# Second attention: scores from two float32r parts, two heads in the two halves of the rows

## The chip, the core and the metric

The kernel runs on one core of one Trainium2 chip, in one launch. The metric is the device time of that launch in microseconds; less is better. Before the change it is 2244.51 us (median of 3 runs, 2242.51 to 2246.36).

## What is computed

Four residual blocks run on a tensor of 4 x 1024 tokens x 128 features. The third, which the change touches, is causal attention with 16 heads of 8 dimensions; the others are a gated memory (before it) and two feed-forward blocks with local attention (one before it, one after).

```python
x = x + attn_a(_layernorm(x)); x = x + ffn(_layernorm(x))
x = x + attn_b(_layernorm(x)); x = x + ffn(_layernorm(x))

def attn_b(x):                        # 4 x 1024 x 128, H = 16 heads, DK = 8
    Q, K, V = (split_heads(x @ W.T) for W in (Wq, Wk, Wv))
    Q, K = apply_rope(Q, cos, sin), apply_rope(K, cos, sin)
    logits = einsum('bhnd,bhmd->bhnm', Q, K) / sqrt(DK)
    probs = softmax(where(causal, logits, -inf), axis=-1)
    attn = einsum('bhnm,bhmd->bhnd', probs, V)
    return merge_heads(attn) @ Wo.T
```

The scores are large enough that queries and keys rounded once to bf16 would not do; softmax also needs each row's maximum.

## The kernel before, in words

`network` runs five stages one behind the other; the second attention is `attn_b_stage`, from 893 to about 1502 us of the profiled execution. Its engines have a program each, joined by semaphores.

**Parts.** The projections and the rotation give f32 queries and keys, 128 rows (16 heads x 8 dimensions) x 1024 tokens for each of 4 batches. Each value is split into three bf16 parts (`PARTS = 3`): ACT copies to bf16 (`first_part`), DVE or POOL subtracts (`remainder`), ACT copies again (`second_part`), DVE or POOL subtracts again (`third_part`). The parts go to DRAM (`store_parts`, `store_first_rows`) and come back (`load`) so that all nine products of parts are rows of one contraction: `KS9` = 3 x 3 x 8 = 72 rows of `QS` and `KS`. Three more rows hold the three bf16 parts of minus the row maximum in `QS`, and ones in `KS`, so that 75 rows give score minus maximum.

**Steps.** Work goes in 16 groups (`NG`) of 4 heads (`BG`). Step n has eight slots j, one for each tile of 128 keys. In slot j four things run side by side:

- exponentials (`exp_unit`, L1684): scores of keys tile j against queries from tile j on, transposed, into one of two buffers of 1024 columns (`s2_ps`); ACT takes exp of it into `PT` (L1867). A group has 22 such units.
- values (`value_block`, L1702): `PT` of slot j-1 times [V, 1], f32, four heads in four column groups of 32, in one or two halves of 512 queries. For n < 3 the causal cut is a mask matmul ahead of the scores (L1679); from n = 3 (`SELECTS`) POOL cuts in `PT` (L2080), and the value block waits for it.
- maxima for a later group (`max_unit`, L1652): scores of one query tile against its keys, at most 512 columns, into one of two banks (`s1_ps`); DVE reduces each with max (L1956). The causal cut is a mask matmul of 128 columns ahead of the scores (L1649). A group has 38 units. `MAX_TILES` puts query tiles 4, 7, 6, 5 in slots 0 to 3 and 3, 2, 1, 0 in slots 4 to 7.
- offsets: after slot 3 DVE joins the two halves of the maxima (`maximum`), POOL splits them in bf16 parts in four operations (`offsets`), in slot 5 PE turns them (`turn_unit`, L1661), DVE copies them to `MT`, and one DMA on SP writes the three rows of `QS` (`rows`, L1532). The first exponential of the next step waits for it.

Each engine runs its instructions in the order in which the loops write them. On PE, `step` spreads a slot's maxima evenly behind its exponentials and value blocks (`some_maxima`); a maximum that waits for its bank holds back every exponential and value block behind it. SP issues the outputs' DMAs (`store_out`, two times eight a step), `rows` and, once a group is done, `load` of the group three ahead (`RING` = 3), six DMAs.

## Time and profile before

| | |
|---|---|
| runs | 2242.51, 2244.51, 2246.36 us, median 2244.51 |
| the profiled execution | span 2242.3 us from the first to the last instruction |
| its granted TensorE clock | 0.973 of 2.4 GHz on average |
| second attention | 893 to about 1502 us |
| first exponential, last step | 980.2 us, 1465.4 us |

The span is the profiled execution's own time as far as the profile records it; what lies around it is not in the profile, and the median of the runs is 2.2 us above it. An engine's busy time is what its instructions took; matmuls overlap, and a matmul's recorded duration includes its latency, so PE's pace is read from the starts. PEclk is the granted clock, 1.00 for 2.4 GHz and 0.50 for 1.2 GHz.

### The profile page before, as it was taken

The page shows a single profiled execution, that of the slowest core. Times are in us where ns is not written, and L with a number is a line of the kernel's source. Part 1 is how long each engine was busy: PE and PEld are TensorE (multiplying, and loading weights), DVE is VectorE, ACT ScalarE, POOL GpSimd, SP SyncE. Part 2 cuts the span into 40 slices and gives each one's busy share as a digit, 9 for nine tenths or more (in the row PEclk, how much of TensorE's full clock was granted, in tenths as well). Part 3 has the DMA queues.
Part 4 walks back from the last instruction along what each step waited for, and adds up shares of the span by engine and source line. Part 5 has one row for each costly group of instructions (what it writes and reads, how often), then busy time and mean ns, then how long its engine had stood idle before and what let it go on. Part 6 is the DMA issues. An engine that isn't in the chain of part 4 may idle for free. (4 is left out here: it accounts for less than half of the span.)

```text
span 2242.3 us, 44709 instructions
## 1 busy us (share of the span) xinstructions
PE 2064.8 (92%) x16567; PEld 1059.9 (47%) x16567; DVE 1792.0 (80%) x2386; ACT 1390.5 (62%) x3475; POOL 1233.3 (55%) x633
## 2 busy tenths in 40 slices
PE   5677899999999997899999999967999999999997
PEld 2224555555555553443333333314555555555554
DVE  6986889899899993666777777717899899899993
ACT  8455566666666664446666666665666756766663
POOL 0217777777777772135121221128777787777770
PEclk9899999999999999889999999999999999999998
DMA  2004112112112110402111111113111111111111
GB/s 62 0 6 121 35 34 47 35 34 48 35 36 47 35 34 19 130 29 88 55 48 52 54 36 46 32 55 87 31 43 42 35 44 39 34 44 39 35 34 43
DMA packets 86075, 101.14 MB, mean 45 GB/s; under 512 B 13817, under 2 KB 59841, under 8 KB 83557
## 3 DMA queue, kind: packets, MB, share of 16 engines
q1 hardware_dynamic: 83429, 96.58, 16.8%
q8 instruction: 135, 2.21, 0.4%
q10 hardware_dynamic: 2432, 1.70, 0.3%
q14 instruction: 79, 0.65, 0.1%
HBM read 35.98 MB, written 8.39 MB: 20 GB/s over the span
## 5 line engine op out<-in xcount | busy, mean ns | idle before, releaser
L831 POOL TENSOR_TENSOR ffn_RN<-ffn_SS,ffn_mhalf 128x16 f32<-128x16 f32 x128 | 372.5, 2910 | 279.3 <-DVE ffn_SS L777 278.9
L1956 DVE TENSOR_REDUCE attn_b_NX<-attn_b_s 128x1 f32<-128x512 f32 (+3 forms) x608 | 381.3, 660 | 132.0 <-PE attn_b_s L1652 126.8
L825 POOL TENSOR_TENSOR ffn_QK<-ffn_T 128x1024 f32<-128x1024 f32 x128 | 421.6, 3294 | 17.6 <-DVE ffn_T L725 17.4
L576 ACT ACTIVATE ffn_PB<-ffn_s,ffn_NM 128x128 f32<-128x128 f32 x1024 | 360.8, 386 | 101.1 <-DVE ffn_NM L747 101.1
L1867 ACT ACTIVATE attn_b_PT<-attn_b_s 128x1024 f32<-128x1024 f32 (+3 forms) x352 | 298.2, 870 | 192.4 <-PE attn_b_s L1684 188.0
L612 ACT ACTIVATE ffn_SQ<-ffn_w 128x1024 f32<-128x1024 f32 x128 | 131.2, 1025 | 312.0 <-DVE ffn_T L725 311.7
L819 POOL TENSOR_TENSOR ffn_PB<-ffn_PB,ffn_RDEN 128x1024 f32<-128x1024 f32 x128 | 243.7, 1904 | 25.1 <-DVE ffn_RDEN L710 25.1
L367 PE MATMUL ffn_w<-ffn_Wqkv,ffn_H 128*128 128x512 f32 x512 | 244.2, 600 | 10.4 <-ACT ffn_SQ L612 4.7
L576 ACT ACTIVATION_READ_ACCUMULATOR ffn_PB<-ffn_s,ffn_NM 128x1 f32 x1024 | 231.0, 226 | 0.0
L1652 PE MATMUL attn_b_s<-attn_b_KS,attn_b_QS 72*128 72x512 bf16 (+3 forms) x768 | 220.6, 336 | 6.2 <-DVE attn_b_NX L1956 5.5
L741 DVE TENSOR_TENSOR ffn_QK<-ffn_QK,ffn_RN 128x1024 f32<-128x1024 f32 x128 | 222.4, 1738 | 0.4 <-POOL ffn_RN L831 0.3
L764 DVE COPY ffn_PT<-ffn_w 128x1024 f32<-128x1024 f32 x128 | 156.2, 1220 | 76.1 <-PE ffn_w L421 72.6
L2080 POOL TENSOR_SCALAR_AFFINE_SELECT attn_b_PT<-attn_b_PT 128x512 f32<-128x512 f32 x104 | 66.8, 642 | 252.6 <-ACT attn_b_PT L1867 251.4
L1684 PE MATMUL attn_b_s<-attn_b_QS,attn_b_KS 75*128 75x512 bf16 (+3 forms) x768 | 186.9, 333 | 5.9 <-ACT attn_b_PT L1867 4.8
L442 PE MATMUL ffn_m<-ffn_HN,ffn_W 128*114 128x512 f32 x360 | 185.9, 613 | 6.4 <-ACT ffn_G L596 3.7
L722 DVE TENSOR_TENSOR ffn_T<-ffn_w,ffn_rope 128x1024 f32<-128x1024 f32 x128 | 154.8, 1210 | 36.6 <-PE ffn_w L367 36.4
L1702 PE MATMUL attn_b_o<-attn_b_PT,attn_b_VQ 128*32 128x512 f32 (+3 forms) x1536 | 166.2, 505 | 3.8 <-POOL attn_b_PT L2080 3.5
L725 DVE TENSOR_TENSOR ffn_T<-ffn_w,ffn_rope 128x512 f32<-128x512 f32 x256 | 163.7, 681 | 0.0
L747 DVE TENSOR_REDUCE ffn_NM<-ffn_s 128x8 f32<-128x1024 f32 x128 | 155.6, 1215 | 9.6 <-PE ffn_s L409 9.6
L774 DVE TENSOR_REDUCE ffn_SS<-ffn_SQ 128x16 f32<-128x1024 f32 x128 | 154.6, 1208 | 2.2 <-ACT ffn_SQ L612 2.2
L437 PEld LDWEIGHTS ffn_w<-ffn_PT,ffn_Voff 128*64 128x64 f32 x2048 | 107.3, 137 | 100.7 <-issue 94.4
L421 PEld LDWEIGHTS ffn_w<-ident,ffn_PB 128*128 128x128 f32 x1024 | 117.4, 143 | 75.4 <-issue 60.5
(257 smaller groups left out, 3756.4 us busy)
## 6 DMA issues: line engine op xcount, KB each, us to landing
ffn_Voff<-ffn_Vcur SPq DMA_DIRECT2D x248, 128.0 KB, 2.3
attn_b_QS<-attn_b_qk_parts SPq DMA_DIRECT2D x48, 192.0 KB
attn_b_KS<-attn_b_qk_parts SPq DMA_DIRECT2D x48, 192.0 KB
ffn_H<-ffn_Y SPq DMA_DIRECT2D x64, 128.0 KB, 2.5
ffn_H<-ffn_U SPq DMA_DIRECT2D x64, 128.0 KB, 2.5
attn_b_qk_parts<-attn_b_RP SPq DMA_DIRECT2D x6, 768.0 KB, 4.3
ffn_rope<-in_ffn_rope_dram SPq DMA_DIRECT2D x4, 1024.0 KB, 7.9
attn_b_rope<-attn_b_OS SPq DMA_DIRECT2D x252, 16.0 KB
```

Of the source, the lines that this page charges most:

```text
L367: last = pe.matmul(w0_ps[:, c, :], H1[:, g % 2, b, :], Wqkv[:, l, c, :], start=True, stop=True)
L442: pe.matmul(mlp_bank(g, half, j), W1[:, g // NT, half, j, :], HN[:, :], start=True, stop=True)\
L576: last = act.activation(PB[:, x % 2, e, p, :], s_ps[:, e, p * P:(p + 1) * P], ACT.Exp, bias=NM[:, x % 2, e, p:p + 1], accum_out=DEN[:, x % ...
L741: dve.tensor_tensor(qk, qk, RN[:, x % 2, :].unsqueeze(2).broadcast_to([P, 2 * NH, DH]), ALU.mult)\
L819: pool.tensor_tensor(probs_x, probs_x, by, ALU.mult).then_inc(normed, 1)
L825: pool.tensor_tensor(QK[:, x % 2, :, :, :].rearrange("p c q k -> p (c q k)"), T1[:, :, :, :].rearrange("p c h k -> p (c h k)"), T2[:, :, : ...
L831: pool.tensor_tensor(RN[:, x % 2, :], SS[:, x % 2, :], mhalf[:, :], ALU.pow).then_inc(rnorm, 1)
L1652: last = pe.matmul(bank[:, q * width:(q + 1) * width], QS[0:KS9, m % RING, g + q, i * P:(i + 1) * P], KS[0:KS9, m % RING, g + q, lo:hi], s ...
L1684: last = pe.matmul(bank[:, q * pitch + lo:q * pitch + hi], KS[:, n % RING, g + q, j * P:(j + 1) * P], QS[:, n % RING, g + q, j * P + lo:j ...
L1702: last = pe.matmul(o_ps[half][VCOLS * g:VCOLS * (g + 1), lo - half * 512:512], VQ[:, n % 2, g, j, :], PT[:, j % 2, g, lo - j * P:hi - j * ...
L1867: act.activation(PT[:, j % 2, g:g + pack, 0:width], s2_ps[k % 2][:, 0:pack * pitch].rearrange("p (q w) -> p q w", q=pack)[:, :, 0:width], ...
L1956: dve.tensor_reduce(NX[:, m % 2, c, g:g + pack, i], s1_ps[k % 2][:, 0:pack * (hi - lo)].rearrange("p (q w) -> p q w", q=pack), AX_X, ALU.m ...
```

## The change

Queries and keys are split into two parts of 12 bits in the type float32r (`PARTS = 2`): an ACT copy and one subtraction. The four products of parts are 4 x 8 = 32 rows (`TERMS`), and a second head gets the other 64 rows (`NPAR` = 2 halves, `HROWS` = 64, `NPR` = 2 heads in each half, four heads a group as before). Rows 32 to 61 of each half are filled with ones in `KS` and zeros in `QS`; rows 62 and 63 hold the two parts of minus the maximum. The maxima use 62 rows of a half, the exponentials all 64. The causal masks are matmuls on one half of the rows too, two of 64 columns a head where one of 128 was. An exponential's unit is now one half of the queries (512 columns or less) for two or four heads, one bank for each half of the rows: 20 units instead of 22. The maxima keep 38 units. `rows` takes four DMAs, `load` eight. The core of the diff:

```diff
-PARTS = 3
-KS9 = PARTS * PARTS * BD
+PARTS = 2
+TERMS = PARTS * PARTS * BD
+NPAR, NPR = 2, 2
+HROWS = P // NPAR
+OFFSETS = HROWS - PARTS
...
-        RP = sb("RP", [P, 2, PARTS, T], BF16)
+        RP = sb("RP", [P, 2, PARTS, T], F32R)
-        QS = sb("QS", [KS9 + PARTS, RING, BG, T], BF16)
-        KS = sb("KS", [KS9 + PARTS, RING, BG, T], BF16)
+        QS = sb("QS", [P, RING, NPR, T], F32R)
+        KS = sb("KS", [P, RING, NPR, T], F32R)
...
             def rows(m):
                 sp.wait_ge(s1_read, s1_at["turn", m] + 1)
-                sp.dma_start(QS[KS9:KS9 + PARTS, m % RING, :, :].rearrange("a g t -> a (g t)"), MT[:, m % 2, :])\
-                  .then_inc(s_rows[m % 2], 16)
+                for par in range(NPAR):
+                    for a in range(PARTS):
+                        at = par * HROWS + OFFSETS + a
+                        of = (a * NPAR + par) * NPR * NT
+                        sp.dma_start(QS[at:at + 1, m % RING, :, :].rearrange("a q t -> a (q t)").bitcast(F32),
+                                     MT[of:of + NPR * NT, m % 2, :]).then_inc(s_rows[m % 2], 16)
...
+            def mask(at, par, kind, half, n, first):
+                rows = rows_for(par, HROWS)
+                pe.matmul(at, causal[rows, kind, half, 0:P],
+                          causal[rows, kind, half:half + 1, P:P + HROWS].broadcast_to([HROWS, n, HROWS]), start=first,
+                          stop=True, skip_group_check=True)
...
+            def max_unit(m, slot, u):
...
+                if diagonal:
+                    at = bank[:, 0:n * width].rearrange("p (q w) -> p q w", q=n)
+                    for half in range(2):
+                        lo = width - P + half * HROWS
+                        mask(at[:, :, lo:lo + HROWS], par, 0, half, n, half == 0)
+                rows = rows_for(par, OFFSETS)
+                for q, (i, c, pr) in enumerate(segments):
+                    last = pe.matmul(bank[:, q * width:(q + 1) * width], QS[rows, m % RING, pr, i * P:(i + 1) * P],
+                                     KS[rows, m % RING, pr, c * 512:c * 512 + width], start=not diagonal, stop=True,
+                                     skip_group_check=True)
...
+            def exp_unit(n, j, u):
...
                 for q in range(pack):
-                    for lo in range(0, width, 512):
+                    for par in range(NPAR):
+                        rows = rows_for(par, HROWS)
+                        last = pe.matmul(bank[par][:, q * width:(q + 1) * width],
+                                         KS[rows, n % RING, first + q, j * P:(j + 1) * P],
+                                         QS[rows, n % RING, first + q, lo:hi], start=not masked and q == 0, stop=True,
...
-            def second_part(b, w):
-                act.wait_ge(r1, 2 * b + w + 1)
-                act.activation(RP[:, w, 1, :], work_buffers(b, w)[0], ACT.Copy).then_inc(p2, 1)
...
+            for par in range(NPAR):
+                at = par * HROWS + TERMS
+                pool.wait_ge(s_set, 2 * par + 1)
+                pool.memset(KS[at:(par + 1) * HROWS, :, :, :].bitcast(F32), 1.0).then_inc(s_set, 1)
+                pool.wait_ge(s_set, 2 * par + 2)
+                pool.memset(QS[at:par * HROWS + OFFSETS, :, :, :].bitcast(F32), 0.0).then_inc(s_set, 1)
```

## Rows read from the trace of the kernel before

**Rows 1.** The page, part 1: busy us of each engine, share of the span, instructions.

```profile
span 2242.3 us, 44709 instructions
...
PE 2064.8 (92%) x16567; PEld 1059.9 (47%) x16567; DVE 1792.0 (80%) x2386; ACT 1390.5 (62%) x3475; POOL 1233.3 (55%) x633
```

**Rows 2.** Windows of the eight slots of one step: busy us per engine, then PE clock.

```profile
1244.54:1248.74 4.20, 3.86 (x29) 1.41 (x27) 3.38 (x5) 3.56 (x4) 0.56 (x2) 1.00 0.27 68
1248.74:1254.80 6.06, 5.87 (x40) 1.88 (x37) 4.55 (x8) 4.26 (x6) 1.44 (x3) 1.00 0.50 163
1254.80:1260.72 5.92, 5.49 (x37) 1.81 (x36) 4.74 (x9) 3.25 (x4) 0.63 (x1) 1.00 0.10 20
1260.72:1265.65 4.93, 4.75 (x37) 1.71 (x35) 4.27 (x7) 2.71 (x4) 0.63 (x1) 1.00 0.00 0
1265.65:1269.18 3.53, 3.53 (x31) 1.24 (x28) 2.79 (x5) 2.05 (x2) 1.35 (x5) 1.00 0.00 0
1269.18:1272.37 3.19, 2.96 (x22) 1.09 (x21) 1.93 (x5) 2.00 (x3) 0.88 (x2) 1.00 0.01 3
1272.37:1274.52 2.15, 2.15 (x19) 0.97 (x18) 1.69 (x3) 1.02 (x1) 0.46 (x2) 1.00 0.20 38
1274.52:1275.90 1.38, 1.38 (x19) 0.73 (x17) 0.69 (x1) 0.60 (x1) 0.50 (x2) 1.00 0.13 24
```

**Rows 3.** Timeline of PE, slot 1: start us, us, line, tiles, form, [idle].

```profile
1250.03 1.06 PE L1702 MATMUL attn_b_o<-attn_b_PT,attn_b_VQ 128*32 128x512 f32 x8
1251.03 0.61 PE L1652 MATMUL attn_b_s<-attn_b_KS,attn_b_QS 72*128 72x512 bf16 x2
...
1252.20 0.23 PE L1649 MATMUL attn_b_s<-attn_b_causal,identb 128*128 128x128 bf16 x1 [0.19 <-DVE attn_b_NX L1956]
1252.27 0.38 PE L1652 MATMUL attn_b_s<-attn_b_KS,attn_b_QS 72*128 72x512 bf16 x1
```

**Rows 4.** Timeline of DVE at the same place, with its idle time.

```profile
1251.45 2.58 DVE L1956 TENSOR_REDUCE attn_b_NX<-attn_b_s 128x1 f32<-128x512 f32 x4 [0.63 <-PE attn_b_s L1652]
```

**Rows 5.** Timeline of ACT, slot 0.

```profile
1245.18 3.77 ACT L1867 ACTIVATE attn_b_PT<-attn_b_s 128x1024 f32<-128x1024 f32 x4 [1.00 <-PE attn_b_s L1684]
```

**Rows 6.** Groups of instructions from 893 to 1502 us: busy, mean ns, idle.

```profile
L1956 DVE TENSOR_REDUCE attn_b_NX<-attn_b_s 128x1 f32<-128x512 f32 (+3 forms) x608 | 381.3, 660 | 132.0 <-PE attn_b_s L1652 126.8
```

**Rows 7.** Timeline of PE in the feed-forward stage before.

```profile
701.16 0.41 PE L400 MATMUL ffn_s<-ffn_masks,identb 64*64 64x512 bf16 x4
...
706.28 1.88 PE L367 MATMUL ffn_w<-ffn_Wqkv,ffn_H 128*128 128x512 f32 x4
```

**Rows 8.** Tile view of the score banks: weight loads, min/median/max ns.

```profile
L1652 PEld LDWEIGHTS attn_b_s<-attn_b_KS,attn_b_QS x768: 95/98/152, 931.4 to 1457.7; 72*128 72x128 bf16 x192
...
L1591 PEld LDWEIGHTS attn_b_s<-attn_b_XN,attn_b_W x64: 186/190/337, 900.6 to 969.5; 128*128 128x128 f32 x64
...
L1661 PEld LDWEIGHTS attn_b_s<-identb,attn_b_NP x16: 119/119/123, 975.6 to 1460.5; 128*96 128x96 bf16 x16
```

**Rows 9.** Windows where the clock fell: PE, PEld, DVE, ACT, POOL, PEclk.

```profile
972.00:976.00 4.00, 2.78 (x18) 1.23 (x16) 3.00 (x6) 1.09 (x2) 3.77 (x7) 0.99 0.00 0
976.00:980.00 4.00, 3.73 (x16) 1.43 (x17) 3.03 (x6) 0.00 (x0) 3.92 (x2) 0.50 0.03 6
1048.00:1052.00 4.00, 3.35 (x29) 1.59 (x27) 2.69 (x4) 3.15 (x4) 2.72 (x2) 1.00 0.14 25
980.00:1012.00 32.00, 31.47 (x188) 12.18 (x186) 21.70 (x36) 18.66 (x22) 4.59 (x7) 0.80 0.01 1
1045.00:1077.00 32.00, 30.43 (x213) 12.05 (x210) 21.50 (x35) 20.00 (x25) 9.45 (x8) 0.89 0.30 96
```

**Rows 10.** Timeline of the SP queue after one offset turn.

```profile
1270.75 0.78 SPq L1532 DMA_DIRECT2D attn_b_QS<-attn_b_MT  x1
```

**Rows 11.** The page, part 6: DMA issues, KB each, us to landing.

```profile
ffn_Voff<-ffn_Vcur SPq DMA_DIRECT2D x248, 128.0 KB, 2.3
```

**Rows 12.** Timeline of POOL at the stage's start.

```profile
893.87 1.80 POOL L2015 MEMSET attn_b_VQ<- 128x2048 f32 x1
```

More of the change, by code:

```diff
@@ L12 @@
 F32 = mybir.dt.float32
+F32R = mybir.dt.float32r
 BF16 = mybir.dt.bfloat16
@@ L1448, in last_max, with last_exp @@
         def last_max(m):
-            i, c, g, pack = max_units(MAX_SPLIT - 1)[-1]
-            return s1_at[m, i, c, g]
-        def last_exp(n, j):
-            return s2_at[n, j, exp_heads(j)[-1][0]]
+            slot = MAX_SPLIT - 1
+            return s1_at[m, slot, len(max_units(slot)) - 1]
+        def last_exp(n, j, half=1):
+            return max(s2_at[n, j, u] for u, unit in enumerate(exp_units(j)) if unit[0] <= half)
         def work_buffers(b, w):
@@ L1669, in exp_unit @@
+                pe.matmul(s1_ps[k % 2][0:PARTS * BG * NT, 0:P],
+                          NP[:, m % 2, :, :, :, :].rearrange("p a g h i -> p (a g h i)").bitcast(F32),
+                          keep["ident"][:, :], start=True, stop=True).then_inc(s1_mm, 1)
+            def exp_unit(n, j, u):
+                k = s2_at[n, j, u]
+                half, first, pack = exp_units(j)[u]
+                lo, hi = piece(j, half)
+                width = hi - lo
                 wait(pe, probs, k - 1)
-                if (n, j, g) == (0, 0, 0):
+                if (n, j, u) == (0, 0, 0):
@@ L1671, in exp_unit @@
                     pe.wait_ge(held, 4 * (NB - 2))
-                if (j, g) == (0, 0):
-                    pe.wait_ge(s_rows[n % 2], 16 * (n // 2 + 1))
-                each = max(1, 512 // pitch)
-                selected = n >= SELECTS
-                for q in range(0, 0 if selected else pack, each):
-                    at = bank[:, q * pitch:q * pitch + each * min(pitch, 512)]\
-                        .rearrange("p (q w) -> p q w", q=each)[:, :, 0:P]
-                    pe.matmul(at, keep["identb"][:, :], causal[:, 1:2, :].broadcast_to([P, each, P]), start=True,
-                              stop=True)
@@ L1724, in step @@
                     halves = list(range(j // 4, 2)) if 0 <= v < NG else []
-                    pieces, done = len(heads) + len(halves), 0
+                    pieces, done = len(exps) + len(halves), 0
                     def some_maxima(done):
-                        for unit in scores[len(scores) * done // pieces:len(scores) * (done + 1) // pieces]:
-                            max_unit(m, *unit)
+                        for u in range(len(scores) * done // pieces, len(scores) * (done + 1) // pieces):
+                            max_unit(m, slot, u)
@@ L1738, in step @@
                             value_block(v, j, halves[0])
                             done = some_maxima(done)
-                        if halves and k == len(heads) - 1:
+                        if halves and u == len(exps) - 1:
                             value_block(v, j, halves[-1])
                             done = some_maxima(done)
-                    if not heads:
-                        for unit in scores[:1]:
-                            max_unit(m, *unit)
+                    if not exps:
+                        for u in range(len(scores))[:1]:
+                            max_unit(m, slot, u)
@@ L1746, in step @@
                         if slot == TURN_SLOT and n == -1:
                             turn_unit(0)
-                        for unit in scores[1:]:
-                            max_unit(m, *unit)
+                        for u in range(len(scores))[1:]:
+                            max_unit(m, slot, u)
                             if m == 0:
@@ L1798, in hold @@
                 else:
[L1799 removed]
+                    act.wait_ge(lower, 2 + w + 1)
                 for i in range(2):
@@ L1821, in _ @@
             first_part(0, 1)
-            for w in range(2):
-                second_part(0, w)
             for c in range(4, 6):
@@ L1834, in _ @@
             hold(2, 0)
-            for w in range(2):
-                second_part(1, w)
             hold(2, 1)
@@ L1871, in _ @@
+                if pack > 1:
+                    bank = bank.rearrange("p r (q w) -> p r q w", q=pack)
+                    out = out.rearrange("p (q r) w -> p r q w", r=NPAR)
+                act.activation(out, bank, ACT.Exp).then_inc(probs, 1)
             for n in range(NG):
                 for j in range(NT):
-                    for g, pack in exp_heads(j):
-                        exp_unit(n, j, g, pack)
-                        if (j, g) == (1, 0) and n >= 1:
+                    for u in range(len(exp_units(j))):
+                        exp_unit(n, j, u)
+                        if (j, u) == (1, 0) and n >= 1:
@@ L1942, in _ @@
             remainder(1)
-            for w in range(2):
-                third_part(w)
             for c in range(4, NCH):
@@ L2045, in parts_of @@
                     remainder(b, w)
-                for w in range(2):
-                    third_part(b, w)
             def values(m):
```

291 lines of the change are left out of this document (147 added, 144 removed).

## Prediction, made before the changed kernel was run

> **What bounds the kernel now.** Read the page first [rows 1]: the span is 2242.3 us, PE is busy 92% of it and DVE 80%. That average is over stages the change does not touch, so the next views are of the second attention alone, 893 to 1502 us. Cut one step of it at the starts of its eight slots and the windows give 4.20, 6.06, 5.92, 4.93, 3.53, 3.19, 2.15 and 1.38 us, 31.36 us in all [rows 2]. PE is busy 29.99 us of these, DVE 24.05, ACT 19.45. Busy PE means little, as overlapping ends are counted; what counts is from start to start. The timeline shows two score matmuls of 512 columns started in 0.44 us, 0.22 each; a causal mask of 128 columns takes 0.07 before its score matmul starts; a value block (eight f32 instructions, four heads in four column groups) takes 1.00 us [rows 3]. By these, a step's 36 tiles of 128 columns times 4 heads are 18432 columns, at 2.4 GHz 7.7 us for the maxima and 7.7 us for the exponentials; masks 22 x 0.07 and more for wide ones, some 1.8; value blocks 9.5: 512 columns in four passes are 0.85 us of the 1.00, and with the other 0.15 kept the narrower ones take 0.79, 0.58 and 0.36 (six, two, two and two of them). For the turn into each of the 12 blocks I put 0.1, an estimate from that 0.15: 1.2. Sum 27.9 of 31.36: PE is close to its limit, and DVE (38 reductions, 0.66 us mean [rows 6]) close behind. The engines are coupled: the maxima have two banks, and while PE is in a value block DVE runs dry. It waits 0.63 us after one [rows 4]; in slots 1 to 3 DVE is busy 13.56 of 16.91 us, so 3.35 us is such waiting. Slot 0 is different: four exponentials of 1024 in 3.77 us [rows 5] fill the 4.20 us, so ACT sets it.
>
> **The change, part by part.**
> The exponentials' scores (L1684). 48 matmuls a step stay 48, but neighbours work on different halves of the rows and on different banks. Whether halves overlap is seen one stage earlier: four 64x512 matmuls on quarters of the array start within 0.24 us, where one alone needs 0.21 [rows 7]. So a pair takes one matmul's time, and 7.7 us becomes 3.85. The float32r rate is in no row. Ends: the bf16 row, 0.22 us for 512 columns [rows 3]; and f32, where two products of 512 columns take four instructions and 1.88 us [rows 7], some 0.9 each with the last one's latency, four times bf16. 
>
> The maxima's scores (L1652). Still 38 units and 48 matmuls, each unit one half of the rows. Two units overlap only when both banks are free, which DVE seldom lets happen: I take no gain (0 to 3.8 us a step).
>
> Weight loads. A 128-column bf16 load lasts 95 ns, a 96-column one 119, an f32 one 186 [rows 8]: 128 columns of bf16 are loaded faster than fewer. If a float32r load loses that, it adds about 40 ns, half the distance from 95 to 186. Beside a 512- or 256-column matmul this is hidden; beside 64-column masks and 128-column matmuls it isn't. Each diagonal maximum now has two masks of 64 columns a head in place of one of 128, so another load too. I take 55 ns for each diagonal unit, between nothing and 2 x 70 (two mask rows [rows 3]); slots 4 to 7 have 12 of them, and slot 7 has one unit more than before: 13 x 0.055 = 0.7 us. In slots 1 to 3 the ten others lie beside DVE.
>
> The Trainium skill, "TensorE: Matmul & The Clock Gate" (LDWEIGHTS, and Weight-path perf modes), speaks against the change: a load takes its columns over 1.2 GHz, 107 ns, with the fast form for none of the 4-byte types. A pair of 512 columns then needs 214 ns of loads beside 213 ns of columns, so pairs of 384, 256 and 128 columns also take 214: the exponentials would take 24 x 0.214 = 5.1 us, not 3.85, and the gain per step be 1.2 us smaller. The 24 ns between the 96- and the 128-column load agree that bf16 has a faster form; what a float32r load costs, no row shows.
>
> Slot by slot. Slot 0: ACT still has four of 1024, 4.20 to 4.10. Slots 1 to 3: each wait of DVE behind a value block had an exponential's matmuls in it, and PE now arrives earlier at the block. What is left is the block's 1.00 plus about 0.4 us to the first new maximum, less the two maxima that DVE holds, of which one is begun: about 0.4 us where it was 0.63. Six blocks then leave 2.05 us of the 3.35: gain 1.3, ends 0 and 3.35. Slots 4 to 7: PE sets them (busy 10.02 of 10.25 us); the exponentials have 4 x (512 + 384 + 256 + 128) = 5120 columns, 2.13 us, half goes: 1.07 less 0.7 for masks and loads, gain 0.37. Together 0.1 + 1.3 + 0.37 = 1.77 us a step. The 15 steps that still have maxima beside them make 26.5 us; the last one is set by ACT, with 20 exponentials in place of 22, and I take nothing.
>
> ACT and DVE. The same 18432 columns in 20 instructions instead of 22: under 0.4 us of ACT a step, not on the path but in slot 0. DVE keeps 38 reductions. The second minimum is smaller, the turned offsets are 64x128 f32 instead of 96x128 bf16: nothing.
>
> The offsets' way. One DMA becomes four on SP. It is issued in 0.78 us at 1270.75 [rows 10]; the next step's first exponential, which waits for it, starts near 1275.9, 5.2 us on. Such a transfer inside the chip lands 2.3 us after its issue [rows 11]; the last of four then lands at 0.78 x 3 + 2.3 = 4.6 us, beside about 5.0 in the shorter slots. Nothing, ends 0 and 1 us a step. Queued behind them on SP are eight DMAs of outputs and the loads, eight instead of six of nearly equal bytes (2 x 64 rows x 8 KB against 2 x 72 rows x 8 KB); these are needed over ten microseconds later. POOL's offset work goes from four operations to two: hidden before, hidden now.
>
> Lead-in. Second and third parts go: eight ACT copies, two DVE and six POOL subtractions. PE and the norm's chain set the time there, and DVE has slack, so nothing, ends 0 and -3 us. New are four memsets of 6144 elements on 30 or 32 rows: at 1.80 us for 2048 [rows 12] 5.4 us each, 21.6 in series, done by about 918, before POOL's first other work at 923. Nothing, ends 0 and +3. The stored parts grow from 768 to 1024 KB each; nobody waits that closely.
>
> Sum: 2242.3 - 26.5 = 2215.8 us of span. The median of the runs is 2.2 us over this span, which I take to lie around it, giving 2218.
>
> **The rivals.**
> The clock falls. A PE that starts its columns sooner and then waits for DVE and ACT is less active, above all in slot 0: four pairs (0.9), four maxima (0.9) and a value block (0.4) in 4.1 us. The clock went to 1.2 GHz after stretches with waits here: 972 to 976 us has PE busy 2.78 of 4 and the next four have 0.50; 1048 to 1052 has 3.35 of 4 at ACT's pace, and the 32 us around it have a mean of 0.89 against 1.00, so 7.0 us at half; 980 to 1012 has 0.80, 12.8 us at half [rows 9]. Then PE sets the pace and loses half of that, 3.5 to 6.4 us for a fall. Against it: no fall in the steady steps before, and pairs use all the rows. It decides from a fall in half of the steps (1.77 / 3.5) on; one in each step gives 15 x (3.5 - 1.77) = +26, 2270, and with 6.4 +69, 2314.
>
> Short float32r matmuls are slow. If those of 128 columns cost as f32, 0.16 us more each: eight maxima and eight exponentials in four pairs a step, up to 12 x 0.16 = 1.9 us, ten of them (1.6) in slot 7 where nothing covers it. 15 x (1.6 - 1.77) = -3: 2242. For: f32's price by column; against: nothing.
>
> Float32r takes more passes. With two, 3.85 us more for the exponentials than forecast, 7.7 for the maxima: PE needs 27.9 - 3.85 + 11.5 + 0.7 = 36.3 us a step, +4.9 x 15 = 74: 2318; with four some 2650.
>
> The halves don't overlap (the change does not do what it says): PE's sum stays at 27.9, plus 0.7 + 0.3: +15, 2260. Against it the quarters [rows 7].
>
> **How the numbers follow.** Forecast 0.52; clock 0.22; short ones 0.12; passes 0.08; no overlap 0.06. About 0.2% (4.5 us) is what a measurement of this kernel tells from none. The forecast is faster for 0.50 and same for 0.02; the clock rival slower for 0.15, same 0.03, faster 0.04; short ones faster 0.05, same 0.04, slower 0.03; the last two slower for 0.13, same 0.01. Faster 0.59, same 0.10, slower 0.31. The forecast's own range is 2196 (3.2 us a step) to 2236. The whole range goes on to 2280 and leaves out the passes, the clock at its dearest and a gain over 3.2 us a step.
>
> **What would show it.** In the changed trace: pairs of L1684's successor starting together, 0.21 us apart from the next; float32r forms of 512 columns lasting as the bf16 ones; loads near 135 ns; steps of about 29.6 us; DVE's waits halved and its 38 reductions unchanged; PEclk 1.00 in the steady steps; no wait of slot 0 for the offsets' DMA. A PEclk of 0.5 in every step, a third column of matmul time on 128-column forms, or a step above 31.4 us would make it wrong.

## The result, and the profile after

The changed kernel takes 2319.11 us, the median of four runs from 2296.53 to 2330.83; the kernel before took 2245.44 beside it. The ratio is 1.0302, 95% interval 1.0271 to 1.0333: slower by 3%, where 2218 was forecast and 2280 was the upper end. The rows of "after" are of the slowest of its runs: 2330.83 us, span 2329.1, mean clock 0.937. The fastest run had a span of 2294.8 at 0.957; the spread goes with the clock.

The page after: busy time of each engine, and the groups of DVE's reductions and ACT's exponentials (busy us, mean ns, idle us before them).

```profile
PE 2103.7 (90%) x16998; PEld 1112.5 (48%) x16998; DVE 1793.5 (77%) x2383; ACT 1378.6 (59%) x3435; POOL 1235.7 (53%) x599
...
L1974 DVE TENSOR_REDUCE attn_b_NX<-attn_b_s 128x1 f32<-128x512 f32 (+3 forms) x608 | 384.0, 660 | 210.8 <-PE attn_b_s L1677 205.2
...
L1892 ACT ACTIVATE attn_b_PT<-attn_b_s 128x1024 f32<-128x1024 f32 (+1 forms) x320 | 292.5, 940 | 279.0 <-PE attn_b_s L1710 276.9
```

The 608 reductions are the same, 660 ns each, but DVE stood idle before them 210.8 us instead of 132.0 [rows 6], almost all of it for the maxima's scores. PE's busy time has risen by 39 us although the two halves' matmuls overlap. So something makes PE later, and the windows say what. A step is cut here from one copy of the turned offsets to the next. First the 15 steps of after in one line, then single steps of it; the columns are those of [rows 9].

```profile
982.08:1544.91 562.83, 499.28 (x3671) 220.56 (x3671) 370.23 (x608) 294.38 (x341) 99.91 (x149) 0.83 0.16 40
...
1134.47:1169.86 35.39, 30.38 (x240) 13.32 (x240) 24.24 (x40) 19.20 (x23) 5.93 (x11) 0.90 0.16 39
...
1242.13:1285.45 43.32, 39.43 (x240) 16.69 (x240) 24.48 (x40) 19.14 (x23) 5.97 (x11) 0.65 0.13 32
1285.45:1318.94 33.49, 28.30 (x240) 12.68 (x240) 24.32 (x40) 19.14 (x23) 5.97 (x11) 1.00 0.17 41
```

And the 15 steps of before:

```profile
975.90:1460.89 484.99, 464.95 (x3268) 170.93 (x3268) 366.60 (x609) 301.03 (x375) 115.14 (x183) 0.98 0.17 48
```

The steps take 77.8 us more, of 86.8 in the whole span (the lead-in 6.2 more, the rest what comes behind). There are two losses. **Pace:** at a clock of 1.00 a step takes 33.2 to 33.5 us (35.5 in the two that also hold a batch's output projection, 33.3 before), where it took 31.4. That is 2 us a step, 30 in all. **Clock:** eleven of the 15 steps contain a stretch at 1.2 GHz. By 562.83 x (1 - 0.83) x 2 it is 191 us of half clock, against some 20 before. One step at 0.65 takes 9.8 us more than its neighbour at 1.00, one at 0.90 takes 2. That leaves the clock some 48 of the 77.8 us, as what the pace doesn't take; in a run of the median time it is some 12 us less.

The slots of one step at full clock, from windows in the manner of [rows 2], for before, for before with half of the exponentials' columns left out (experiment 3), for after, and for after in bf16 (experiment 2):

| slot | 0 | 1 | 2 | 3 | 4 | 5 | 6 | 7 | sum |
|---|---|---|---|---|---|---|---|---|---|
| before | 4.20 | 6.06 | 5.92 | 4.93 | 3.53 | 3.19 | 2.15 | 1.38 | 31.36 |
| before, half the columns | 3.76 | 5.99 | 5.92 | 4.90 | 3.44 | 3.18 | 2.15 | 1.23 | 30.57 |
| after | 3.87 | 6.43 | 6.45 | 4.93 | 4.18 | 3.72 | 2.10 | 1.80 | 33.48 |
| bf16 in halves | 3.54 | 6.14 | 5.97 | 4.52 | 3.74 | 3.24 | 2.05 | 1.51 | 30.71 |

Four of these windows of after:

```profile
1291.29:1295.16 3.87, 2.82 (x26) 1.38 (x24) 2.32 (x5) 3.00 (x4) 0.28 (x1) 1.00 0.13 24
1295.16:1301.59 6.43, 5.87 (x45) 2.39 (x43) 4.99 (x8) 4.75 (x6) 1.56 (x3) 1.00 0.50 129
...
1312.97:1317.15 4.18, 3.50 (x34) 1.22 (x31) 3.45 (x6) 2.05 (x2) 1.28 (x4) 1.00 0.01 2
...
1322.97:1324.77 1.80, 1.80 (x29) 1.30 (x25) 1.20 (x3) 0.60 (x1) 0.42 (x2) 1.00 0.12 22
```

Against before, slot 0 of after gained, every other slot but 3 and 6 lost, and no engine is full in most of them: in slots 4 and 5 PE is busy 6.66 of 7.90 us, DVE 5.45. PE, DVE and ACT wait for one another in turn. The timeline of PE shows what makes a turn longer. First after, then the bf16 version at the same place of a step:

```profile
1477.63 0.50 PE L1710 MATMUL attn_b_s<-attn_b_QS,attn_b_KS 64*128 64x512 f32 x2 [0.88 <-ACT attn_b_PT L1892]
1477.97 0.40 PE L1677 MATMUL attn_b_s<-attn_b_KS,attn_b_QS 62*128 62x512 f32 x1
...
1485.67 0.49 PE L1677 MATMUL attn_b_s<-attn_b_KS,attn_b_QS 62*128 62x512 f32 x2
1485.99 0.40 PE L1710 MATMUL attn_b_s<-attn_b_QS,attn_b_KS 64*128 64x256 f32 x4
1486.93 0.50 PE L1677 MATMUL attn_b_s<-attn_b_KS,attn_b_QS 62*128 62x512 f32 x1 [0.54 <-DVE attn_b_NX L1974]
```

```profile
1150.46 0.39 PE L1677 MATMUL attn_b_s<-attn_b_KS,attn_b_QS 62*128 62x512 bf16 x2
1150.68 0.39 PE L1710 MATMUL attn_b_s<-attn_b_QS,attn_b_KS 64*128 64x256 bf16 x4
1151.62 0.39 PE L1677 MATMUL attn_b_s<-attn_b_KS,attn_b_QS 62*128 62x512 bf16 x1 [0.55 <-DVE attn_b_NX L1974]
```

The pair of the two halves is one line, x2, in 0.50 us: both ran together, so the halves do overlap. A matmul whose load was done before it started takes 0.40, as one of bf16 (0.38 in [rows 3]): the columns run at the bf16 rate. But one that follows a wait takes 0.50, where bf16 takes 0.39, and its load is recorded as starting with it. Experiments 2, 5 and 13 test whether the 0.11 us are this load. In the step of 33.49 us, 50 of the 96 score matmuls are recorded at least 0.05 us longer than any of their form in bf16, in 32 places when neighbours are counted together: 6 right after an idle PE, 4 after a value block, 17 after a mask, the rest after another matmul. PE itself is idle for over 0.06 us only 12 times in that step. The loads of after, on PEld:

```profile
1475.57 0.30 PEld L1677 LDWEIGHTS attn_b_s<-attn_b_KS,attn_b_QS 62*128 62x128 f32 x2
1475.68 0.29 PEld L1710 LDWEIGHTS attn_b_s<-attn_b_QS,attn_b_KS 64*128 64x128 f32 x2
1475.79 0.30 PEld L1677 LDWEIGHTS attn_b_s<-attn_b_KS,attn_b_QS 62*128 62x128 f32 x2
...
1477.63 0.19 PEld L1710 LDWEIGHTS attn_b_s<-attn_b_QS,attn_b_KS 64*128 64x128 f32 x2 [1.31 <-ACT attn_b_PT L1892]
...
1485.64 0.20 PEld L1677 LDWEIGHTS attn_b_s<-attn_b_KS,attn_b_QS 62*128 62x128 f32 x2
```

The profile writes float32r as f32. One float32r load lasts 0.18 to 0.19 us. Two on the same half take 0.30, so they follow each other 0.11 us apart; two on different halves fit in 0.19 or 0.20. The 0.11 us agree with the Trainium skill, "TensorE: Matmul & The Clock Gate" (LDWEIGHTS, and Weight-path perf modes): a load takes its columns over 1.2 GHz, and FP32 has no fast form. Float32r behaves here as the Trainium skill has it for FP32.

### The profile page after: what moved, and what is told of

Same layout as the page of the kernel before. It is cut to its first block and busy times, and to the rows that moved or that the text cites. A ratio compares the mean times of both kernels' runs of the same rounds, so it can differ in the third digit from the quotient of the medians.

```text
span 2329.1 us, 45562 instructions
## 1 busy us (share of the span) xinstructions
PE 2103.7 (90%) x16998; PEld 1112.5 (48%) x16998; DVE 1793.5 (77%) x2383; ACT 1378.6 (59%) x3435; POOL 1235.7 (53%) x599
## 5 line engine op out<-in xcount | busy, mean ns | idle before, releaser
L1974 DVE TENSOR_REDUCE attn_b_NX<-attn_b_s 128x1 f32<-128x512 f32 (+3 forms) x608 | 384.0, 660 | 210.8 <-PE attn_b_s L1677 205.2
L1892 ACT ACTIVATE attn_b_PT<-attn_b_s 128x1024 f32<-128x1024 f32 (+1 forms) x320 | 292.5, 940 | 279.0 <-PE attn_b_s L1710 276.9
L1677 PE MATMUL attn_b_s<-attn_b_KS,attn_b_QS 62*128 62x512 f32 (+3 forms) x768 | 267.1, 464 | 22.3 <-DVE attn_b_NX L1974 21.8
L1710 PE MATMUL attn_b_s<-attn_b_QS,attn_b_KS 64*128 64x512 f32 (+3 forms) x768 | 193.4, 432 | 15.7 <-ACT attn_b_PT L1892 15.6
L1727 PE MATMUL attn_b_o<-attn_b_PT,attn_b_VQ 128*32 128x512 f32 (+3 forms) x1536 | 197.5, 591 | 5.2 <-POOL attn_b_PT L2091 5.1
L1677 PEld LDWEIGHTS attn_b_s<-attn_b_KS,attn_b_QS 62*128 62x128 f32 x768 | 126.5, 214 | 100.3 <-DVE attn_b_NX L1974 79.2
```

The source lines that it names most:

```text
L1677: last = pe.matmul(bank[:, q * width:(q + 1) * width], QS[rows, m % RING, pr, i * P:(i + 1) * P], KS[rows, m % RING, pr, c * 512:c * 512 + ...
L1710: last = pe.matmul(bank[par][:, q * width:(q + 1) * width], KS[rows, n % RING, first + q, j * P:(j + 1) * P], QS[rows, n % RING, first + q ...
L1727: last = pe.matmul(o_ps[half][VCOLS * g:VCOLS * (g + 1), lo - half * 512:512], VQ[:, n % 2, g, j, :], PT[:, j % 2, g, lo - j * P:hi - j * ...
L1892: act.activation(out, bank, ACT.Exp).then_inc(probs, 1)
L1974: dve.tensor_reduce(at, bank, AX_X, ALU.max, negate=True).then_inc(s1_read, 1)
```

## The experiments

Each ran beside the kernel before, whose median was 2244.0 to 2246.2 us. "Step" is a step at full clock without an output projection unless its clock is given. A fence under an experiment is one step of it, with the columns as above. The steps are of the one profiled run, the times of all its runs.

**1. Score matmuls of the exponentials run twice** (nothing else is changed).

```diff
-                for q in range(pack):
+                for q in [*range(pack)] * (1 if masked or n < SELECTS else 2):
```

> The changed kernel with every score matmul of the exponentials issued twice in groups 3 to 15 (the second pass overwrites the first with the same values): 3.8 us of matmul more in each of 13 steps. Theory 'clock' (the changed kernel's steps are slow because PE is idle more and the clock is at 1.2 GHz for about 187 us of the stage): PE is active again, the clock stays at 1.00 in nearly all steps after the third, and although it does more work the kernel gets faster, 2265 to 2290 us. Theory 'loads' (each float32r matmul costs more, the clock is a side effect): the extra matmuls and loads add 1.5 to 4 us a step, 2335 to 2370 us.

2292.8 us (2285.49 to 2308.54), ratio 1.0217 [1.0171, 1.0263]: 26 us less than the changed kernel, with 48 more matmuls a step.

```profile
1224.17:1258.21 34.04, 31.26 (x288) 16.39 (x288) 24.41 (x40) 19.22 (x23) 5.96 (x11) 1.00 0.17 40
```

In the profiled run (2286.66 us) the step is longer by half a microsecond to 0.9 us, and every step from the third on is at 1.00; two of the four runs were 12 to 22 us longer at a lower mean clock. So part of the loss is the clock's, and more matmuls on PE take it back. With 'loads' alone the time would have risen.

**2. The changed kernel in bf16** (two bf16 parts in the same halves, rows and order; the scores then carry 16 bits only).

```diff
-F32R = mybir.dt.float32r
+F32R = mybir.dt.bfloat16
...
```

> The changed kernel with the two parts in bf16 in place of float32r (the scores carry 16 bits and no more), the same halves of rows, masks and units; half the bytes in the loads. Theory 'loads': a bf16 weight load is hidden again, steps at a clock of 1.00 take 30 us or less instead of 33.3. Theory 'clock': PE is even less busy, so the falls stay or grow: a mean clock in the steps of 0.85 or less, and the kernel stays slower than before, 2260 to 2310 us. If loads were all of it: 2200 to 2225 us.

2235.21 us (2232.06 to 2236.23), ratio 0.9949 [0.9934, 0.9964], 0.5% faster than before.

```profile
1135.75:1166.46 30.71, 25.06 (x239) 7.76 (x237) 23.65 (x42) 21.29 (x27) 5.97 (x11) 1.00 0.12 28
```

The type costs 2.4 to 2.8 us a step (with it go half of the loads' bytes and the f32 turn of the offsets). Nearly all falls of the clock go too, although PE is busy less here; that part of the expectation missed.

**3. The kernel before with half of the columns of the exponentials' scores** (from group 3 on; it leaves the other half of these scores out).

```diff
+                        if selected:
+                            hi = lo + (hi - lo) // 2
```

> The kernel before with only the first half of the columns of each score matmul of the exponentials computed from group 3 on: leaves out half of these scores. It takes PE time out as the change does (3.8 us a step) but keeps bf16, 75 rows, one mask a unit, all waits. Theory 'clock': less work for PE brings falls of the clock here too, PEclk under 0.95 in the steps and a time of 2250 us or more, although work was taken away. Theory 'loads': the clock stays at 1.00 and 13 steps gain 1.5 to 2 us each: 2215 to 2225 us.

2236.6 us (2232.82 to 2239.61), ratio 0.9958 [0.9943, 0.9972].

```profile
1112.22:1142.79 30.57, 27.37 (x217) 10.39 (x215) 23.78 (x41) 19.40 (x25) 6.49 (x13) 1.00 0.17 50
```

This is the gain of the change without anything else of it: 3.8 us of columns out of PE shorten a step by 0.8 us, and slots 4 to 7, which lose 1.07 us of columns, by 0.25. The time is neither of the two that I had put. The forecast had 2.47 for this alone: its 1.77 and the 0.7 that it charged for masks and loads. The clock stayed, on 72 and 75 rows.

**4. The maxima's mask as one matmul on all rows** in place of two on a half.

```diff
-                    for half in range(2):
-                        lo = width - P + half * HROWS
-                        mask(at[:, :, lo:lo + HROWS], par, 0, half, n, half == 0)
+                    pe.matmul(at[:, :, width - P:width], keep["identb"][:, :],
+                              lower_mask[:, :, :].broadcast_to([P, n, P]), start=True, stop=True)
```

> The changed kernel with the maxima's causal cut as before the change: one mask matmul of 128 columns over all 128 rows, in place of two of 64 columns on one half of the rows. 22 matmuls and loads fewer a step, but PE turns between all rows and half the rows ahead of and behind each diagonal unit. If the doubled masks are what made a step at full clock 2 us longer, such steps take 32.3 us or less instead of 33.3. If the float32r loads are, they stay within 0.5 us of 33.3, or get longer by the turns. Total 2290 to 2330 us by both, as the clock's falls stay.

2421.94 us (2410.45 to 2440.08), ratio 1.079 [1.0736, 1.0845].

```profile
1326.76:1383.10 56.34, 54.80 (x218) 21.84 (x218) 25.23 (x41) 19.29 (x22) 5.95 (x11) 0.50 0.10 25
...
1523.50:1559.45 35.95, 33.50 (x218) 14.82 (x218) 24.82 (x41) 19.14 (x23) 6.00 (x11) 1.00 0.16 39
```

Fewer matmuls (218 for 240), yet 2.5 us more at full clock, some 0.11 for each of the 22 masks. In its trace a score matmul starts 0.16 us behind such a mask, where it is 0.07 in the changed kernel, and its load starts no earlier. The Trainium skill, "TensorEngine Tiling (Array Packing)" (Key Properties), says that a change of the tiling mode drains the engine; the run agrees. The clock fell further too (three steps at 0.50 throughout), so the whole is some 90 us over the 2290 to 2330 that I had put. The changed kernel's split masks were the better choice.

**5. The maxima's 512-column matmuls in two of 256** (24 more float32r loads a step, each beside columns).

```diff
-                    last = pe.matmul(bank[:, q * width:(q + 1) * width], QS[rows, m % RING, pr, i * P:(i + 1) * P],
+                    step_by = 256 if width == 512 else width
+                    for x in range(0, width, step_by):
+                        last = pe.matmul(bank[:, q * width + x:q * width + x + step_by],
...
```

> The changed kernel with each 512-column score matmul of the maxima issued as two of 256 columns: same columns, 24 float32r weight loads more in a step (for 512-column segments). Theory 'loads' (a float32r matmul's weight load, 0.18 us recorded against 0.095 for bf16, is not hidden and costs about 0.11 to 0.13 us each): a step at full clock goes from 33.4 to 35 us or more, and the total by 20 us or more beyond 2319. Rival 'columns' (the loads are hidden, float32r columns stream slower than bf16): steps at full clock stay at 33.4 within 0.5.

2320.71 us (2297.7 to 2323.76), ratio 1.0312 [1.0262, 1.0362]; step 33.20 us, as in the changed kernel. A load beside 256 columns costs nothing that can be seen. So loads in general are not the price of the type; what is left is the load that nothing covers.

**6. Experiment 2 with half of the exponentials' columns from group 3 on** (these scores left out).

```diff
+                        cut = width if n < SELECTS else width // 2
-                        last = pe.matmul(bank[par][:, q * width:(q + 1) * width],
+                        last = pe.matmul(bank[par][:, q * width:q * width + cut],
...
```

> The bf16 variant of the halves with only the first half of the columns of each exponential's score matmul computed from group 3 on (leaves out half of these scores): 1.9 us of PE's columns less a step. Theory 'density' (the clock falls in the changed kernel because the same columns are spread over steps of 33.4 instead of 30.7 us, so PE computes less of the time): taking columns out brings the falls to bf16 too, PEclk 0.95 or less in several steps, total 2240 to 2290. Rival 'type' (float32r matmuls themselves bring the falls): the clock stays near 1.00, steps stay near 30.6, total 2228 to 2236.

2313.78 us (2311.63 to 2314.51), ratio 1.0302 [1.0286, 1.0317].

```profile
1144.47:1184.02 39.55, 33.76 (x239) 9.21 (x237) 24.29 (x42) 21.24 (x27) 6.00 (x11) 0.61 0.09 22
```

Less work than in experiment 2 and 79 us more time, with the clock down to 0.54 to 0.95 in all 12 steps that it changes. So in these halves the clock falls with fewer columns in bf16 too, and further than I had put (2240 to 2290).

**7 and 8. The filled rows left out**, in float32r and in bf16: 33 and 35 rows of each half in the scores instead of 62 and 64.

```diff
-OFFSETS = HROWS - PARTS
+OFFSETS = TERMS + 1
...
-                        rows = rows_for(par, HROWS)
+                        rows = rows_for(par, OFFSETS + PARTS)
```

> The changed kernel with 33 rows of each half for the maxima and 35 for the exponentials (offsets moved down to rows 33 and 34), instead of 62 and 64. If the filled rows do nothing, steps and clock are as in the changed kernel, 2297 to 2331 us. If they keep the clock up, the clock is lower in every step, a mean in the steps of 0.75 or less, and the time is 2350 us or more.

> The kernel with the halves in bf16, with 33 and 35 rows of a half in the scores in place of 62 and 64 (the filled rows are left out, nothing else). 'Filled rows hold the clock up' whatever the type: the clock falls in most steps, steps of 40 us or more, 2370 to 2500 us. 'It was float32r's': the time stays near 2235 us.

2532.91 us (2530.41 to 2534.73), ratio 1.1278 [1.1261, 1.1295], and 2430.69 (2425.62 to 2438.24), ratio 1.0821 [1.0795, 1.0847]. One step of each kernel:

```profile
1229.78:1279.64 49.86, 46.58 (x240) 20.27 (x240) 24.66 (x40) 21.58 (x27) 5.95 (x11) 0.50 0.12 28
```

```profile
1372.51:1416.99 44.48, 40.95 (x239) 10.42 (x237) 24.40 (x42) 21.42 (x28) 5.92 (x11) 0.50 0.08 19
```

Every step ran at half clock or close to it (0.50 to 0.53, and 0.50 to 0.62 in bf16). Where the clock is up, a bf16 matmul of 512 columns lasts 0.37 to 0.39 us on 33, 35, 62 or 64 rows, so the rows of zeros and ones cost no time; leaving them out costs about 14 us a step in bf16, by the clock.

**9. Half-width kernel with all three bf16 parts** (six of the nine products of parts: 48 rows, 13 filled, three of offsets; the three smallest products are left out).

```diff
-PARTS = 2
-TERMS = PARTS * PARTS * BD
+PARTS = 3
+TERMS = PARTS * (PARTS + 1) // 2 * BD
```

> Two heads in the two halves of the rows, but with three bf16 parts as before the change and six of their nine products (the three smallest left out): 48 rows, filled to 61, and three offset rows. By 'loads', steps like the bf16 variant's, 30.7 us at full clock, and the clock up: 2230 to 2242 us, faster than the kernel before (2245) with all three parts kept. If the halves as such are what costs, 2260 us or more.

2238.78 us (2236.19 to 2243.68, seven runs), ratio 0.9972 [0.9961, 0.9984] to before; step 30.71 us, four with a short fall. The change's packing without its type is 0.3% faster than the kernel before.

**10. One more load behind each wait of experiment 2** (32 columns on the same weights, 38 maxima and both halves of 20 exponentials).

```diff
+                pe.matmul(bank[:, 0:32], QS[rows, m % RING, pr, i * P:(i + 1) * P],
+                          KS[rows, m % RING, pr, c * 512:c * 512 + 32], start=True, stop=True, skip_group_check=True)
...
```

> The kernel with the halves in bf16 (steps of 30.71 us at full clock, where the float32r kernel needs 33.2 to 33.5), with one more matmul of 32 columns on the same weights behind every wait for a bank: at the start of each of the 38 maxima and, from group 3 on, of each exponential's two halves. So each wait is followed by a bf16 load of some 95 ns more, about what a float32r load (182 to 188 ns) has over a bf16 one. 'The exposed load' (the 2.5 us of a full-clock step that float32r costs are its longer load behind each wait, 0.11 us by 24): the step becomes 32.5 to 33.5 us, the time 2255 to 2275 us. 'Something else of float32r' (its products, its change of type with the bf16 masks): the added load hides as the added loads beside columns did, 30.7 to 31.2 us, 2235 to 2243 us. Both if the clock stays; a fall adds to either and the full-clock steps alone then decide.

2245.46 us (2242.07 to 2247.3), ratio 0.9994 [0.9985, 1.0003]; step 31.30 us, 0.59 more. Neither theory gave that. PE behind one wait:

```profile
1386.68 0.19 PE L1670 MATMUL attn_b_s<-attn_b_KS,attn_b_QS 62*128 62x32 bf16 x1 [0.50 <-DVE attn_b_NX L1981]
1386.72 0.37 PE L1680 MATMUL attn_b_s<-attn_b_KS,attn_b_QS 62*128 62x512 bf16 x1
```

The score matmul starts some 0.03 us (28 ns before rounding) behind the added one, so the added matmul with its load, recorded with 92 ns, holds the next up for a third of that; whether the 28 ns are its load or the least distance of two matmuls, no run here separates. 0.59 / 0.028 is 21 delays on the path: the added delay does lengthen the step, and my unit was wrong, the record's length for what the next matmul loses.

**11 and 12. No causal masks in the maxima**, in float32r and in bf16 (it leaves the causal cut out of the maxima).

```diff
-                diagonal = c * 512 + width == (i + 1) * P
+                diagonal = False
```

> The changed kernel without the causal masks of its maxima (848 matmuls less; it leaves the causal cut out of the maxima). 'The exposed load': a full-clock step goes from 33.2 or 33.5 to about 32.5 us, as its bf16 counterpart of the same run does by the same amount, and 2 us or more stay between the two types, since most waits are at maxima without a mask. 'The change between bf16 masks and float32r scores': the two types come within 1 us of each other. 'Density': the masks kept columns in the gaps, so without them the clock falls at least as much, and the whole time stays above 2300 us.

> The kernel with the halves in bf16, without the causal masks of its maxima (it leaves the causal cut out of the maxima); the counterpart of the float32r kernel without them. 'The exposed load': its full-clock step goes from 30.71 to about 30 us. 'Change of type': also about 30, and the float32r one comes within 1 us of it. 'Density': PE's 25.06 us of a step become some 24, less than in the kernel with half of the exponentials' columns left out (which fell), so the clock falls here too and the time is over 2260 us; if the clock stays, the time is about 2222 us and density by busy time alone is wrong.

(The first has 704 matmuls less, 44 in each of 16 groups, not 848.) 2300.63 us (2285.46 to 2314.34), ratio 1.026 [1.0219, 1.03], and 2226.26 (2224.73 to 2232.84), ratio 0.9914 [0.9895, 0.9933]. One full-clock step of each:

```profile
1364.39:1396.58 32.19, 27.04 (x196) 11.36 (x197) 24.22 (x41) 19.15 (x23) 5.97 (x11) 1.00 0.18 43
```

```profile
1132.00:1161.67 29.67, 23.86 (x195) 6.29 (x193) 23.45 (x41) 21.27 (x27) 5.97 (x11) 1.00 0.12 28
```

The masks cost 1 us a step in either type, and 2.5 us stay between the types, so the change between bf16 masks and float32r scores is not the cause. The bf16 one has small falls (0.94 or 0.95 in four steps) and not the long ones I expected. The float32r one ran at half clock about as long as the changed kernel: by span and mean clock 187 to 278 us of the execution, against 197 to 293.

**13. Four loads behind each wait of experiment 2** (four matmuls of 2 columns; otherwise as 10).

```diff
+                for _ in range(4):
+                    pe.matmul(bank[:, 0:2], QS[rows, m % RING, pr, i * P:(i + 1) * P],
+                          KS[rows, m % RING, pr, c * 512:c * 512 + 2], start=True, stop=True, skip_group_check=True)
...
```

> The kernel with the halves in bf16, with four more matmuls of 2 columns on the same weights behind every wait for a bank (38 maxima, and from group 3 on both halves of 20 exponentials). One such matmul put the score matmul behind a wait off by 0.028 us and made the step 0.59 us longer; a float32r load puts it off by 0.11 us, four times that. 'The exposed load, 0.11 us by some 21 waits': the step becomes 33.0 to 33.3 us at full clock, as in the float32r kernel. On the clock: 'the waits thin out the columns' says that at the float32r kernel's pace the clock falls as there, several steps of 35 us and more, 2290 to 2330 us; 'float32r itself lowers the clock' says that nearly all steps stay at full clock, 2268 to 2280 us.

2299.38 us (2292.39 to 2304.83), ratio 1.0235 [1.0204, 1.0266].

```profile
1124.16:1168.76 44.60, 42.83 (x559) 17.52 (x553) 24.97 (x41) 19.20 (x24) 5.98 (x11) 0.62 0.08 19
...
1241.28:1274.62 33.34, 30.09 (x559) 14.97 (x553) 24.35 (x42) 19.09 (x23) 5.97 (x11) 1.00 0.11 27
```

Without any float32r in the scores, this has the changed kernel's full-clock step (33.34; 35.5 with the output projection), and falls in ten of 15 steps, at 0.95 or less. Here the first of the four matmuls starts 0.113 us ahead of what follows: 2.63 / 0.113 is 23 delays on the path. The loss of pace follows from a delay at the start of each unit. Of the clock's loss about half does: by span and mean clock the executions have on average 191 us of half clock, where experiment 2 has 126 and the changed kernel 251. The other half stays unexplained.

**14 and 15. Experiment 1 in slot 0 alone, and in slots 1 to 3 alone** (8 and 24 more matmuls a step).

```diff
-                for q in [*range(pack)] * (1 if masked or n < SELECTS else 2):
+                for q in [*range(pack)] * (1 if masked or n < SELECTS or j > 0 else 2):
...
-                for q in [*range(pack)] * (1 if masked or n < SELECTS else 2):
+                for q in [*range(pack)] * (1 if masked or n < SELECTS or j not in (1, 2, 3) else 2):
```

> The changed kernel with the exponentials' score matmuls run twice in slot 0 only (eight more a step, from group 3 on). 'Slot 0 decides the clock' (PE is busy 2.82 of its 3.87 us, waiting for ACT): nearly all steps stay at full clock at about 33.5 us, 2272 to 2285 us, as good as doubling in all slots or better. 'The whole step decides': eight matmuls of the forty-eight do little, steps of 35 to 43 us remain, 2295 to 2325 us.

> The changed kernel with the exponentials' score matmuls run twice in slots 1 to 3 only (24 more a step, from group 3 on), slot 0 as it was. 'Slot 0 decides the clock': falls stay, steps of 35 to 43 us, 2300 to 2330 us. 'The whole step decides': half of the added work of the kernel with all doubled, most falls gone, 2280 to 2300 us.

2303.45 us (2285.98 to 2304.21), ratio 1.0237 [1.0192, 1.0282], and 2297.09 (2295.88 to 2298.5), ratio 1.023 [1.0197, 1.0262]. The profiled run of the first is its fastest: every step from the third to the 14th at 1.00, 33.62 us; the other three took 17 to 18 us more, which is not in a profile. The second had five steps at 0.95 and steps of 33.15 between them. Both medians lie below the changed kernel's 2319, though the first one's interval touches its, and above experiment 1 with all slots doubled (2293). So neither slot 0 nor slots 1 to 3 decide the clock alone.

**16. Experiment 9 with slot 0's score matmuls run twice.**

```diff
-                for q in range(pack):
+                for q in [*range(pack)] * (1 if masked or n < SELECTS or j > 0 else 2):
```

> The kernel with three bf16 parts and six products in halves (2238.8 us, three or four steps with a short fall), with the exponentials' score matmuls of slot 0 run twice from group 3 on. 'Slot 0 decides the clock': the falls after group 3 go, steps of 30.7 to 30.9 us, 2232 to 2237 us. 'The whole step decides', or slot 0 becomes longer by the added 0.21 us a pair: 2237 to 2250 us.

2238.98 us (2237.01 to 2244.18, ten runs), ratio 0.9968 [0.9956, 0.998]. The falls after group 3 are gone, and each step is 0.23 us longer (30.94); the two cancel, and experiment 9 isn't improved.

## Why the prediction was wrong

**The exponentials' scores, 3.85 us out of PE: right.** Pairs start together and columns run at the bf16 rate; a float32r matmul of 128 columns takes 0.22 us where its load is covered, as in bf16. The rivals of more passes, of slow short matmuls and of halves that don't overlap are out.

**The term that failed first: "weight loads ... if a float32r load loses that, it adds about 40 ns", charged to slots 4 to 7 alone, while "in slots 1 to 3 the ten others lie beside DVE".** I weighed loads as a throughput, which columns hide (right, experiment 5), and only beside masks. The price sits where nothing covers a load: when PE takes up work again after a wait for DVE or ACT, after a value block, or after a short mask, the load is 0.11 us longer than in bf16, not 0.04. That is 2.5 us a step over all slots where 0.7 was put, masks included; experiment 2 measured it and 13 rebuilt it from bf16. The two dozen places on the path are 2.63 / 0.113 from 13, not a count in the trace. DVE was not a cover: it is an engine that waits. It is idle for 9.2 us of the step of 33.49, where it was 7.3 of 31.36; behind the first value block of slot 1 it is 0.73 us, where it was 0.63 [rows 4] and I had put 0.4:

```profile
1298.39 2.62 DVE L1974 TENSOR_REDUCE attn_b_NX<-attn_b_s 128x1 f32<-128x512 f32 x4 [0.73 <-PE attn_b_s L1677]
```

The rule of the Trainium skill, "TensorE: Matmul & The Clock Gate" (LDWEIGHTS), that I set beside the sum was true of the load itself (107 ns by it, 0.11 us here); what I worked out from it, 214 ns of loads for a pair, was not, as the two halves load at the same time (0.19 us for both).

**The gain, "together 1.77 us a step": mis-sized.** Without float32r's delay the halves give 0.65 (31.36 to 30.71), and taking the columns out of the old kernel gives 0.8. (Six blocks at 0.63 less 0.4 would be 1.4 for slots 1 to 3, where 1.3 was written.) Slots 1 to 3, where I expected 1.3, gave 0.28 in bf16; slots 4 to 7, with 0.37 expected, lost 0.29; slot 0 gave 0.66 against 0.1. A busy PE was no proof that PE set the pace: in slots 4 to 7 (busy 10.02 of 10.25 us) of the old kernel, taking 1.07 us of columns out gave 0.25 (the windows of these slots in experiment 3 below), and in slots 1 to 3 half of the columns gave 0.10. What does set these slots, the handovers between the engines being the likely thing, no run takes apart. The maxima's masks cost 1 us a step in the halves; what the old ones cost wasn't measured.

```profile
1138.09:1141.53 3.44, 3.28 (x31) 1.16 (x29) 2.72 (x5) 2.05 (x2) 1.63 (x5) 1.00 0.00 0
1141.53:1144.71 3.18, 2.75 (x22) 1.05 (x21) 1.93 (x5) 2.00 (x3) 0.64 (x1) 1.00 0.01 3
1144.71:1146.86 2.15, 1.95 (x19) 0.89 (x18) 1.69 (x3) 1.02 (x1) 0.63 (x1) 1.00 0.16 29
1146.86:1148.09 1.23, 1.23 (x19) 0.65 (x17) 0.69 (x1) 0.60 (x1) 0.25 (x2) 1.00 0.13 23
```

**The clock, a rival at 0.22 with 2270 to 2314: it happened.** It was named, with slot 0 as its worst place, which experiments 14 and 15 did not bear out as the one place. That its 2314 lies near the 2319 measured is luck in part: it adds 6.4 us of clock a step to a gain of 1.77, where the clock took about 3.2 and the pace lost 2. What failed is "against it: no fall in the steady steps before, and pairs use all the rows": the old kernel held its clock also with fewer columns (experiment 3), but the halves at a slower pace, or with fewer columns, did not (experiments 13 and 6). "3.5 us for a fall" was too much for a short one (2 us) and far too little for the stretches that came, 30 us at half clock for 9.8. What PE did before one, in 4 us windows of after: busy 3.12 of 4 and waiting, then the fall.

```profile
1246.00:1250.00 4.00, 3.12 (x39) 2.05 (x35) 2.74 (x5) 1.77 (x3) 0.85 (x2) 1.00 0.13 25
1250.00:1254.00 4.00, 3.82 (x25) 1.87 (x29) 2.73 (x5) 4.00 (x6) 1.03 (x2) 0.84 0.32 90
1254.00:1258.00 4.00, 3.64 (x19) 1.23 (x16) 1.92 (x3) 1.56 (x2) 0.00 (x0) 0.50 0.53 127
```

**The edits costed at nothing.** The four DMAs of the offsets take 3.23 us on SP, about as worked out; the last lands at 1323.74 us and the next step's first exponential starts at 1324.77, so it does not wait for them, and PE's waits in slot 0 are for ACT; the four memsets took 5.21 us each, as estimated, and ended at 915. The lead-in is 6.2 us longer, 982.1 for 975.9 us; kernels with the same lead-in lie up to 4 us apart there (981.6 to 985.4 in float32r, 975.9 and 978.4 in the old one), and no run here takes the rest apart.

What stays open: what the clock answers to. Columns, filled rows and the pace each moved it, while PE's busy time did not order the kernels (steps at full clock have PE busy 25.06 of 30.71 us in the bf16 one, which held it nearly throughout, and 28.30 of 33.49 in the changed one, which did not). Half of float32r's loss by the clock is not rebuilt by the delays of experiment 13 either.

## What to carry to other kernels

When engines hand small buffers round, price an operation by what it adds where nothing covers it, and count these places. Here 0.11 us in some two dozen of them outweighed what 3.85 us less on PE gave, which was 0.7 or 0.8. Before thinning out a busy PE, ask what keeps the clock: a kernel that is near the edge loses more from a fall than the saving was worth, and filled rows were a way to stay above it that took no time here. And change the layout and the type apart: here the layout alone, in bf16, beat the old kernel by 0.3 to 0.5%, and the type undid it.

## What the runs showed of the hardware

- Float32r matmuls on half the rows run 512 columns in the bf16 time (0.40 and 0.38 us with latency); 128-column loads of it take 182 to 188 ns and follow each other 0.11 us apart, those of bf16 92 to 97 ns. An added bf16 matmul of 32 columns with its load puts off the next by 0.028 us only.
- Loads for the two halves of the rows run at the same time: two float32r ones in 0.19 to 0.20 us, one alone 0.18 to 0.19.
- Leaving out filled rows (62 and 64 to 33 and 35) took the clock in bf16 from 1.00 in most steps to 0.50 to 0.62 in all, the step from 30.71 to 44.48 us, though no matmul is longer for the rows.
- 22 masks on all rows between matmuls on half of them cost 2.5 us a step at full clock, though they replaced 44 smaller ones.
